# Attention and a scaled linear layer on one core: where the maxima, the shifts and the second batch's rotary work stand among the shifted scores, and programs without loops

## What is computed

```python
xn = _layernorm(x, axis=-1)                     # x: 2 x 1024 x 128, fp32
x = x + _L0_attn_ref(xn, wq, wk, wv, wo) + _L0_ffn_ref(xn, CB, SCB, bias)
...
# attention: 16 heads of 8 channels, rotary embedding on Q and K
scores = jnp.einsum('bhqd,bhkd->bhqk', Q, K) * scale
scores = jnp.where(causal_mask, -jnp.inf, scores)
attn = jax.nn.softmax(scores, axis=-1)
out = jnp.einsum('bhqk,bhkd->bhqd', attn, V)
return out.transpose(0, 2, 1, 3).reshape(B, N, D) @ wo.T
...
# ffn
out = jnp.einsum('bsk,nk->bsn', x, CB) * (SCB * (1.0 / 127.0)) + bias
```

## Time and profile before

| | |
|---|---|
| median of 3 runs | 287.1 us (285.83 to 287.21) |
| the profiled execution | 285.84 us, span 284.1 us |
| PE busy | 254.6 us (90%) |
| DVE busy | 217.6 us (77%) |
| ACT busy | 186.5 us (66%) |
| POOL busy | 108.0 us (38%) |
| mean granted PE clock | 0.985 |

### The profile page before, as it was taken

One profiled execution on the slowest core, in us unless ns is written; L12 is line 12 of the kernel. 1 busy time (PEld: TensorE's weight loads), 2 busy tenths in 40 slices (PEclk: granted clock), 3 DMA queues, 4 the chain that ended last, 5 costly groups with the idle time before them and its releaser, 6 DMA issues.

```text
span 284.1 us, 6851 instructions
## 1 busy us (share of the span) xinstructions
PE 254.6 (90%) x1734; PEld 111.1 (39%) x1760; DVE 217.6 (77%) x618; ACT 186.5 (66%) x350; POOL 108.0 (38%) x179
## 2 busy tenths in 40 slices
PE   0695849679999999999999999999999999998984
PEld 0342815333334334432433343334334432464553
DVE  5898368999898888979897898889888979732123
ACT  0326343566778868787777777687868786677851
...
DMA packets 22614, 17.76 MB, mean 63 GB/s; under 512 B 4148, under 2 KB 21940, under 8 KB 22600
## 3 DMA queue, kind: packets, MB, share of 16 engines
...
## 4 chain that ended last, share of the span: by engine, by line
PE 77%; DVE 8%; DMA 4%; SPq 3%; issue 2%; POOL 2%; ACT 1%
PE psV L841 25%; PE psB L817 24%; PE psA L796 21%; DVE prod L665 4%; PE psA L891 3%; DMA k_scratch<-ot 2%; SPq L273 2%; DMA x_sb<-x 1%; DVE xn L623 1%; SPq L287 1%; DMA ks<-k_scratch 1%; PE psA L910 1%; PE psB L778 1%; DVE prod L650 1%; DVE stats L613 1%
## 5 line engine op out<-in xcount | busy, mean ns | idle before, releaser
L665 DVE CUSTOM_DVE_ANT_0 prod<-psA,cmask 128x128 f32<-128x128 f32 (+7 forms) x256 | 180.5, 754 | 34.4 <-PE psA L796 32.9
L564 ACT ACTIVATE ring<-psB 128x512 f32<-128x512 f32 x288 | 156.6, 602 | 53.7 <-PE psB L817 52.5
L796 PE MATMUL psA<-ks,qs 128*128 (+4 forms) x375 | 88.3, 327 | 9.3 <-DVE mx L665 5.9
L433 POOL TENSOR_SCALAR_AFFINE_SELECT ring<-ring 128x512 f32<-128x512 f32 x64 | 42.1, 670 | 138.5 <-ACT ring L564 138.3
L817 PE MATMUL psB<-qs,ks 128*128 (+4 forms) x367 | 92.6, 326 | 1.6 <-issue 1.1
L841 PE MATMUL psV<-ring,va 128*32 128x512 f32 (+3 forms) x768 | 78.5, 496 | 0.6 <-ACT ot L571 0.6
L817 PEld LDWEIGHTS psB<-qs,ks 128*128 (+1 forms) x384 | 33.2, 97 | 69.9 <-issue 28.7
L796 PEld LDWEIGHTS psA<-ks,qs 128*128 (+1 forms) x384 | 33.1, 98 | 40.2 <-DVE mx L665 11.1
L841 PEld LDWEIGHTS psV<-ring,va 128*32 128x32 f32 x768 | 16.8, 108 | 29.7 <-issue 19.2
L665 DVE DVE_READ_ACCUMULATOR2_ANT mx<- 128x1 f32 x256 | 21.3, 83 | 0.0
L713 DVE TENSOR_TENSOR xn<-psA,x_sb 128x256 f32<-128x256 f32 x6 | 2.5, 425 | 16.1 <-PE psA L910 16.1
...
## 6 DMA issues: line engine op xcount, KB each, us to landing
...
q_scratch<-ot SPq DMA_DIRECT2D x20, 128.0 KB, 2.4
k_scratch<-ot SPq DMA_DIRECT2D x12, 128.0 KB, 2.4
...
qs<-shiftsT SPq DMA_DIRECT2D x64, 2.0 KB
y<-xn SPq DMA_DIRECT2D x8, 128.0 KB, 1.8
```

The lines of the kernel that those rows point to most:

```text
L433: pool.affine_select(out=view, in_=view, compare_op=ALU.is_ge, fill=0.0, base=0, pattern=[[0, QUAD], [1, P]], channel_multiplier=-1).then_ ...
L564: act.activation(ring[:, s % P_RING, k * HALF:(k + 1) * HALF], bank_b(n % B_RING), ACT.Exp)\
L665: last = dve.tensor_tensor_reduce(masked_scores[:, u % 2, at:at + w], psA[:, (u % 2) * SEQ + at:(u % 2) * SEQ + at + w], cmask[:, SEQ - w: ...
L796: mm = pe.matmul(psA[:, (u % 2) * SEQ + at + k:(u % 2) * SEQ + at + min(k + HALF, w)], stack(qs, i, j, t * P, P), stack(ks, i, j, k, min(H ...
```

## The change

The maxima of the first quad are cut at its half: 14 of the 22 units stay ahead of body 0, the other 8 go behind banks 2 to 9 of it (`FIRST_UNIT_BANK`), and then the first six units of quad 1 behind bank 9. In later bodies, unit and value tables change, most units of the second half standing in pairs behind three banks. POOL splits a quad's second half behind mask 0 of that quad's own body, where before it was behind mask 8 of the body before; DVE transposes that half two units into the next quad's maxima instead of one, and the first half one unit later. All loops are written out, with constant waits. The second batch's rotary work goes between the masks and exponentials of bodies 0, 1 and 2, the sum of x and ffn in four pieces as well; `store_parts(2)` and `(3)` follow in bodies 1 and 2 on SP. `EARLY` starts at bank 10 of the last body instead of bank 1. Batch 1's second token half is kept in `xnT`.

```diff
@@ -60,9 +60,11 @@
 
 
 
-UNIT_BANK = [1, 2, 4, 6, 7, 9, 10, 12, 14, 15, 15, 19, 20, 21, 23, 24, 25, 26, 27, 30, 32, 34]
-VALUE_BANK = [9, 14, 17, 20, 23, 25, 31, 35, 39, 42]
-LAST_VALUE_BANK = [9, 12, 14, 17, 20, 24, 28, 33, 37, 39]
+UNIT_BANK = [0, 2, 2, 6, 8, 9, 11, 12, 14, 14, 17, 17, 20, 20, 23, 23, 26, 26, 29, 29, 32, 33]
+FIRST_UNIT_BANK = [-1] * 14 + [2, 3, 5, 7, 7, 9, 9, 9]
+VALUE_BANK = [11, 14, 17, 20, 23, 26, 29, 32, 38, 41]
+LAST_VALUE_BANK = [9, 11, 14, 20, 22, 25, 28, 33, 37, 39]
+
...
@@ -76,16 +78,16 @@
 
 
 GROUPS = TILES // 2
-EARLY = {1: 0, 6: 1, 12: 2, 18: 3, 24: 4, 29: 5}
+EARLY = {10: 0, 14: 1, 18: 2, 22: 3, 26: 4, 29: 5}
 TURN_BACK, PROJECT = 4, 6
 
 
 
 
-TASKS = [("late", 4), ("late", 5), ("v", 0), ("v", 1), ("late", 6), ("late", 7), ("ffn", 0), ("ffn", 1)]
+TASKS = [("late", 4), ("late", 5), ("v", 0), ("v", 1), ("ffn", 0), ("ffn", 1), ("late", 6), ("late", 7)]
 FIRST_TASKS = 3
 
-TASK_AFTER = {1: (3, 0), 2: (3, 1), 5: (4, 0), 6: (4, 1), 7: (5, 0), 8: (5, 1), 11: (6, 0), 12: (6, 1), 13: (7, 0), 14: (7, 1)}
+TASK_AFTER = {0: (3, 0), 1: (3, 1), 3: (4, 0), 4: (4, 1), 5: (5, 0), 6: (5, 1), 8: (6, 0), 9: (6, 1), 11: (7, 0), 12: (7, 1)}
 LATE = 4
 
...
@@ -171,8 +173,11 @@
 
         def raw(c, m):
 
-            at = 8 * (c % 2) + 4 * m
-            return xn[:, at:at + 4, :].rearrange("p t d -> p (t d)")
+            if c < LATE + 2:
+                at = 8 * (c % 2) + 4 * m
+                return xn[:, at:at + 4, :].rearrange("p t d -> p (t d)")
+            at = (2 * (c % 2) + m) * HALF
+            return xnT[:, at:at + HALF]
 
         ffn_sb = ot[:, 2:4, :]
...
@@ -236,19 +241,15 @@
         y_filled = sem("y_filled")
         y_ready = sem("y_ready")
         y_out = sem("y_out")
-        passed = sem("passed")
-
-        def wait(eng, semaphore, value, alone=False):
-
-            if isinstance(value, int) and value <= 0:
-                return
-            eng.wait_ge(semaphore, value)
-            if alone and not isinstance(value, int):
-                eng.sem_inc(passed, 1)
-
-        def stacks_loaded(n):
-
...
@@ -310,34 +309,25 @@
             store_parts(1)
             sp.wait_ge(scratch_out[1], 16 * ROUND_DMAS)
             load_stack(0, 1)
-            sp.wait_ge(pads_ready, 2)
-            for hf in range(2):
-                sp.wait_ge(stack_in[hf], stacks_loaded(1))
-                load_stack(1, hf)
+            sp.wait_ge(pads_ready, 4)
+            load_stack(1, 0)
+            load_stack(1, 1)
             store_shifts(0, 0)
-            store_parts(2)
-
-            def body(i):
+            load_stack(2, 0)
+            load_stack(2, 1)
+            store_shifts(0, 1)
+            for i in range(1, QUADS):
+                store_shifts(i, 0)
                 store_shifts(i, 1)
-                if isinstance(i, int):
-                    sp.wait_ge(pads_ready, 4)
-
-                for hf in range(2):
-                    wait(sp, stack_in[hf], stacks_loaded(i + 2), alone=True)
-                wait(sp, b_filled, i * NBANKS, alone=True)
-                for hf in range(2):
-                    load_stack(i + 2, hf)
-                store_shifts(i + 1, 0)
-
-            body(0)
-            store_parts(3)
-            for r in range(2, 4):
-                sp.wait_ge(scratch_out[r], 16 * ROUND_DMAS)
-            with sp.Fori(1, QUADS - 2) as i:
-                body(i)
-            store_shifts(6, 1)
-            store_shifts(7, 0)
-            store_shifts(7, 1)
+                if i in (1, 2):
+                    store_parts(i + 1)
+                if i + 2 < QUADS and i + 2 >= SLOTS:
+                    if i == 2:
+                        for r in range(2, 4):
+                            sp.wait_ge(scratch_out[r], 16 * ROUND_DMAS)
+                    sp.wait_ge(b_filled, i * NBANKS)
+                    load_stack(i + 2, 0)
+                    load_stack(i + 2, 1)
             ov = out.rearrange("(t p) d -> p t d", p=P)
             for g in range(GROUPS):
...
             pads(ks, 1, TWO_ONES, pads_ready)
 
             def third_part(c):
...
 
-            for c in range(LATE):
-                third_part(c)
-                if c == 1:
-                    pool.memset(cmask[:, :], 0.0).then_inc(cmask_ready, 1)
-                    pool.wait_ge(cmask_ready, 1)
-                    pool.affine_select(out=cmask[:, SEQ - P:SEQ], in_=cmask[:, SEQ - P:SEQ],
-                                       compare_op=ALU.is_ge, fill=LOWEST, base=0, pattern=[[-1, P]],
-                                       channel_multiplier=1).then_inc(cmask_ready, 1)
+            third_part(0)
+            third_part(1)
...
@@ -476,17 +442,61 @@
             pool.wait_ge(cb_scaled, 2)
             pool.tensor_tensor(w_sb[:, 6, :], w_sb[:, 6, :], scb_sb[:, :], ALU.mult).then_inc(cb_scaled, 1)
             pool.memset(va[:, :, :, DH:DH + 1], 1.0).then_inc(cb_scaled, 1)
-            rotate(6)
-            rotate(7)
-            leave(6)
-            leave(7)
-            third_part(6)
-            third_part(7)
-            split_maxima(0, 1)
-            body(0, True)
-            with pool.Fori(1, QUADS - 1) as i:
-                body(i, True)
-            body(QUADS - 1, False)
+            split_maxima(0, 0)
+            rotate(4, 0)
+            rotate(4, 1)
+            rotate(4, 2)
+            for i in range(QUADS):
+                wait(pool, pv_done, i * NSTEPS - 3)
+                if i == 0:
+                    pool.wait_ge(task_saved, TASKS.index(("v", 1)) + 1)
+                copy_v(i, 0)
+                mask(i, 0)
+                if i > 0:
+                    split_maxima(i, 1)
+                if i == 1:
+                    third_part(4)
+                if i == 2:
+                    leave(7)
+                mask(i, 1)
+                if i == 1:
+                    third_part(5)
+                if i == 2:
+                    third_part(6)
+                wait(pool, pv_done, i * NSTEPS)
+                copy_v(i, 1)
+                mask(i, 2)
+                if i == 0:
+                    split_maxima(0, 1)
+                if i == 2:
+                    third_part(7)
+                if i + 1 < QUADS:
+                    split_maxima(i + 1, 0)
+                if i == 0:
+                    rotate(5, 0)
+                    rotate(5, 1)
+                    rotate(5, 2)
+                    leave(4)
+                    rotate(6, 0)
+                    rotate(6, 1)
+                if i == 1:
+                    rotate(7, 0)
+                    rotate(7, 1)
+                    rotate(7, 2)
+                    leave(6)
+                    add_ffn(0)
+                    add_ffn(1)
+                mask(i, 7)
+                if i == 0:
+                    leave(5)
+                if i == 1:
+                    add_ffn(2)
+                mask(i, 8)
+                if i == 0:
+                    rotate(6, 2)
+                if i == 1:
+                    add_ffn(3)
+                mask(i, 9)
 
 
         @block.scalar
...
-            save_task(2)
-            save_task(3)
-            parts_of(4, 0)
-            parts_of(5, 0)
-            parts_of(4, 1)
-            parts_of(5, 1)
-            save_task(4)
-            save_task(5)
-            parts_of(6, 0)
-            parts_of(7, 0)
-            save_task(6)
-            save_task(7)
-            parts_of(6, 1)
-            parts_of(7, 1)
+            for n in range(len(TASKS)):
+                save_task(n)
 
             def exps(i, s, then=None):
                 wait(act, pv_done, i * NSTEPS + s - P_RING + 1)
...
-                wait(act, pv_done, i * NSTEPS + LAST[hf] + 1)
-                act.activation(ot[:, bass.ds(i, 1), hf * HALF:(hf + 1) * HALF].rearrange("p o q -> p (o q)"),
-                               psV[:, :], ACT.Copy).then_inc(ot_saved, 1)
-
-            def body(i, first):
+                act.wait_ge(pv_done, i * NSTEPS + LAST[hf] + 1)
+                act.activation(ot[:, i, hf * HALF:(hf + 1) * HALF], psV[:, :], ACT.Copy).then_inc(ot_saved, 1)
+
+            PARTS_AFTER = {(0, 2): (4, 0), (0, 8): (5, 0), (0, 9): (4, 1), (1, 0): (5, 1), (1, 3): (6, 0), (1, 7): (7, 0),
+                           (1, 9): (6, 1), (2, 3): (7, 1)}
+
+            def body(i):
                 for s in range(NSTEPS):
                     exps(i, s)
-                    if s == LAG - 1 and not first:
...
-                    if u == HALF_UNITS + 2:
-                        turn_shifts(i + 1, 0)
-                    maximum(i + 1, u)
-
-            dve.wait_ge(cmask_ready, 2)
-            for u in range(NUNITS):
-                if u == HALF_UNITS + 2:
-                    turn_shifts(0, 0)
-                maximum(0, u)
-            body(0, True)
-            with dve.Fori(1, QUADS - 1) as i:
-                body(i, True)
-            body(QUADS - 1, False)
+                    if u == 2 and i > 0:
+                        turn_shifts(i - 1, 1)
+                    if u == HALF_UNITS + 3:
```

(29 more changed lines are left out.)

156 lines of the change are left out of this document (67 added, 89 removed).

## The result

The changed kernel takes **325.35 us** (median of 4 runs, 322.54 to 327.29) against 286.91 us for the kernel before (4 runs). The ratio is 1.134, with a 95% interval of 1.1251 to 1.1429. I had said 317, with a range of 306 to 330.

What follows compares the result with a forecast made beforehand. PE was taken as the bound in the bodies; 1.9 (body 0) + 18.0 (bodies 1 to 6) + 1.5 (body 2) + 3.8 (last body) + 5 (clock) = 30.2 on 285.84 gives 316.0, said as 317, range 306 to 330.

Steps and rivals of the forecast that it cites:

- The relay: Bank 3 to bank 10, through exponential, mask 0, split, transpose, SP's four issues and landing: 6.9 to 7.0 us each body.
- the landing: Arrival of the last shift DMA before bank 10: taken as 1.1 us behind the end of SP's last issue.
- The unit tables as such give nothing: PE's sum of work is the same: In the bodies, the new unit tables were to change the time by nothing.
- 3.3 - 0.3: Bodies 1 to 6, each: 3.3 us added PE wait for shifts less 0.3 from unrolling, 18.0 us in six bodies.
- So constant waits and no branch are worth 0.3 us a body: Writing out the loops saves 0.3 us a body, read from bank 10 to the next body: 18.77 against 19.06.
- Body 0 ("1.9 us later"): Body 0 starts some 8 us earlier, all lost in waiting for shifts; body 1 starts 1.9 us later than 84.78.
- Body 2 ("1.5"): Body 2: third_part(7) delays the split queued behind it, then DVE's transpose and unit 9; PE waits 1.5 us, between 0 and 2.
- The last body ("+3.8"): Last body and output: +1.8 us from the later bank 10, 2.0 from EARLY's moved work, together +3.8.
- The clock ("+5"): PE's clock falls behind the new gap in about half of seven bodies, 1.4 us each: +5, between 0 and 11.
- the larger wait: Rival: same wait, larger, by a landing near 2.0 or a clock fallen in every body: 323 to 331, chance 0.12.
- what I described: The main case, a wait for the shifts in each body with the summed terms: 312 to 323, chance 0.55.
- hops overlapped: Rival: overlapping hops from bank 3 to bank 10 shorten the wait to 1 to 2 us a body: 290 to 305, chance 0.07.

Runs made afterwards that it cites:

- e1: The changed kernel with only the second half's split moved back between masks 8 and 9 of the body before: 301.61 us, ratio 1.0494, body 27.66 us.
- e5: e1 with UNIT_BANK and VALUE_BANK of the kernel before: 289.4 us, ratio 1.014, body 26.07 us.
- e12: e1 with UNIT_BANK alone as in the kernel before, VALUE_BANK staying new: 301.44 us, ratio 1.048, body 27.62 us.
- e4: The changed kernel, late split kept, with three VALUE_BANK entries (V0, V8, V9) as in the kernel before: 306.92 us, ratio 1.0689, body 28.25 us.
- e3: The kernel before with its five loops written out and constant waits, nothing else: 283.41 us, ratio 0.9882, body 26.07 us.
- e11: e3 run once more, on the same chip as e10: 281.29 us, ratio 0.9814, body 26.07 us.
- e6: e1 with DVE's transpose of the second half behind unit 0 of the next quad instead of unit 1: 300.84 us, ratio 1.0524, body 27.59 us.
- e8: e1 with EARLY and LAST_VALUE_BANK of the kernel before: 300.4 us, ratio 1.0506, body 27.66 us.
- e7: e1 with all units of quad 0 ahead of body 0 and its second split ahead of mask 0: 299.11 us, ratio 1.0466.
- e10: The changed kernel with split, tables, transposes and first quad as before; written-out programs, TASKS and spread POOL and ACT work stay: 287.57 us, ratio 1.0032.

## Why the prediction was right, and where its steps were off

The time lies in the range and the main cost is the one forecast, but the sum came near partly by luck. Forecast were 30.2 us; the profiled executions differ by 41.4, the medians by 38.4.

**The mechanism and the size of the wait: right.** The relay took 6.68 us, forecast 7.0; the last hop, the landing, was 1.24 us behind the end of SP's last issue, forecast 1.1. The Trainium skill, "DMA: Bandwidth & Descriptors", Anatomy of one DMA, by which it would be 1.3 (a figure given for descriptors made by GpSimd), agrees with the 1.24 on SP's queue. Bank 10 waited in each body, with the DMA of `shiftsT` as its releaser. PE was to stand 3.3 us a body; 6.68 less 3.64 of work is 3.0, and its two stands in body 4 add up to 2.63. Undoing the split alone gave back 30.18 - 27.66 = 2.5 us a body, e1.

**"The unit tables as such give nothing: PE's sum of work is the same": failed.** The step looked at sums and not at order. The new value table costs 1.55 us a body without any late split (e5, e12), and with it three of its entries alone cost 1.9 (e4). The term "3.3 - 0.3" a body was 3.0 and came out at 3.62 (30.18 - 26.56): -0.49 for written-out loops (e3), +1.59 for the tables (e1 less e5), +2.52 for the split. The forecast was near because the wait was taken 0.8 too large while the tables stood at nothing.

**"So constant waits and no branch are worth 0.3 us a body": right in sign, mis-sized.** It is 0.49 (e3, e11). The step compared only bank 10 to the next body. That stretch gave 0.23; the stretch from bank 0 to bank 10, which it left out, gave another 0.27. By the Trainium skill, "Runtime: NRT & Kernel Launch", Instruction fetch mechanics, the turns of the loops could give back more than the row of body 0 said. The traces don't show that: the stretch with the branch at its end is the one that gave 0.23. e3 takes away the registers and the branches together, so it doesn't tell the two apart.

**Body 0 ("1.9 us later"): mis-sized.** It was 8.8. DVE's transpose of its second half, and PE's bank 10:

```profile
67.15 0.21 DVE L671 STREAM_TRANSPOSE shiftsT<-shifts 128x32 bf16<-128x32 bf16 x1
```

```profile
71.17 1.01 PE L802 MATMUL psB<-qs,ks 128*128 128x512 bf16 x2 [0.84 <-DMA qs<-shiftsT]
```

- 3.7 came ahead of it: the stack's second half, on which unit 8 waits, came at 45.44 instead of 41.78. In the six experiments with the same beginning (e1, e4, e5, e6, e8, e12) it came at 41.6 to 42.8, so this is more likely one execution's delay than a cost of the change; why it came late is open.
- 1.5 lie between the stack and bank 10. To the transpose it took 21.7 us, 19.2 before, where I had allowed 1.05 more; in e7, with the first quad whole, it takes 19.0. From the transpose bank 10 follows in 4.0 instead of 5.1, near the 4.2 forecast.
- 3.7 lie behind bank 10: 22.43 us to body 1, 18.77 before. An undisturbed body takes 20.18 there, so 1.4 is the new order and 2.3 is this body's own. The clock was at 0.50 in the first 5.6 us of it, worth up to 2.8, a loss that I had put into bodies 1 to 7 only.

The 2.2 us that `leave(5)` costs in e10 are none of this: there body 1 starts as in e11 (84.11 and 84.05), and the loss is at a split which the changed kernel has elsewhere. That the earlier start is lost in the wait for the shifts was right: e7 is no slower.

**Body 2 ("1.5"): right, between 0.9 and 3.8.** `third_part(7)` ahead of the split holds DVE and PE as described. In e10 it cost 3.8 us with the clock's fall behind it; in e5, at a clock of 1.00, the same body took 27.01 us, 0.9 more than its neighbours. In the changed kernel body 2 is 1.1 us longer than body 4 at the same clock, with a stand of 1.03 at a unit.

**The last body ("+3.8"): 6.3.** Bank 10 came 9.1 us into it, forecast 9.6. `EARLY` and `LAST_VALUE_BANK` account for 2.4 by the traces (e8), forecast 2.0. The relay is the larger part, where I had 1.8: without it and with the same tables (e1), the body is 4.1 us shorter from its first exponential to the end (41.05 instead of 45.19). Of these, 2.8 come before bank 10. I had compared with the bank 10 of the kernel before, ahead of which two turns stand that the change moves away, so the relay had more to cost. The other 1.4 come behind it, where the clock fell after a stand of 2.49 us; in e1 it stays at 1.00 there. PE's row, and the window behind it:

```profile
288.41 0.59 PE L802 MATMUL psB<-qs,ks 128*128 128x512 bf16 x1 [2.49 <-DMA qs<-shiftsT]
```

```profile
288.40:292.00 3.60, 3.59 (x23) 1.67 (x23) 0.00 (x0) 1.19 (x2) 0.00 (x0) 0.53 0.00 0
```

**The clock ("+5"): about right in sum, off in place.** At a mean of 0.963 over 325.5 us the clock took 12.0 us, before, at 0.985 over 284.1, 4.3: the change costs 7.8 at most, less what fell into PE's stands. It fell in three of bodies 1 to 7, about half as forecast: bodies 1 and 5, at 0.95, took 2.1 and 1.3 us more than body 4, near the 1.4 that I had taken, and then the last. Bodies 2, 3, 4 and 6 held 1.00. The largest loss is in body 0. It belongs to the interleaved first quad: the seven kernels that have it spend 6.8 to 10.2 us of body 0 at 0.50, e7 and e10, which have it whole, 3.4 around its start.

**The rivals.** 325.35 lies in the band of the larger wait (323 to 331, chance 0.12), above the 312 to 323 of what I described. But neither of that rival's causes is there: the landing is 1.24 us, not near 2.0, and the clock didn't fall in every body. What filled the difference are the tables, body 0 and the last body. No hops overlapped either.
